# Decoder layer on one core: keys and values of a batch projected by shared 512-column products

## What is computed

```python
def attn(h):                                   # h = layernorm(x)
    q, k, v = h @ q_w.T + q_b, h @ k_w.T + k_b, h @ v_w.T + v_b   # split into 16 heads of 16
    qp, kp = elu(q) + 1, elu(k) + 1
    kv = einsum('bhsd,bhse->bhde', kp, v)
    z = einsum('bhsd,bhd->bhs', qp, kp.sum(axis=2))[..., None]
    return merge(einsum('bhsd,bhde->bhse', qp, kv) / (z + EPS)) @ o_w.T + o_b

x = x + attn(layernorm(x))
x = x + softmax(masked context scores * ...) against layernorm(x)
x = x + ffn(layernorm(x))                      # fwht, silu(gate) * up, fwht, down
```

## Time and profile before

| | us |
|---|---|
| median of 3 runs (lowest, highest) | 125.69 (125.47, 125.76) |
| the profiled execution | 125.14 |
| its span in the trace | 123.3 |
| PE busy | 119.2 (97%) |
| DVE busy | 82.7 (67%) |
| ACT busy | 71.6 (58%) |
| POOL busy | 68.5 (56%) |

### The profile page before, as it was taken

The page is one execution under the profiler, slowest core; times in us unless marked ns, Lnnn a source line. Parts: engine busy times, 40 slices in busy tenths (PEclk is TensorE's granted clock), DMA queues, the critical chain, the costliest instruction groups (busy, mean ns, idle before and its releaser), DMA issues.

```text
span 123.3 us, 2272 instructions
## 1 busy us (share of the span) xinstructions
PE 119.2 (97%) x804; PEld 107.0 (87%) x804; DVE 82.7 (67%) x207; ACT 71.6 (58%) x158; POOL 68.5 (56%) x89
## 2 busy tenths in 40 slices
PE   5999999999999999999999999999999999999990
PEld 2259999999999999999989999988888888889890
DVE  1399989899889899899998959674522332220521
ACT  1785696679748689888491479983135444280000
POOL 2228959979979966959802605762005574066000
DMA  3999910280000000000000110000110000000121
GB/s 123 316 377 423 398 76 5 53 330 3 8 0 0 0 5 3 0 0 0 0 5 0 43 45 0 5 0 0 39 46 3 5 0 0 0 0 0 54 73 43
DMA packets 3823, 7.64 MB, mean 62 GB/s; under 512 B 544, under 2 KB 1952, under 8 KB 3684
## 3 DMA queue, kind: packets, MB, share of 16 engines
q1 hardware_dynamic: 3806, 7.50, 16.8%
q10 hardware_dynamic: 6, 0.01, 0.0%
HBM read 6.46 MB, written 1.05 MB: 61 GB/s over the span
## 4 chain that ended last, share of the span: by engine, by line
PE 97%; POOL 0%; DVE 0%; issue 0%; POOLq 0%
PE bank L1283 19%; PE bank L1295 18%; PE bank L1300 11%; PE bank L1177 10%; PE bank L1304 5%; PE bank L1201 5%; PE bank L1239 5%; PE bank L1155 4%; PE bank L1115 4%; PE bank L1211 3%; PE bank L1221 3%; PE bank L1309 2%; PE bank L1146 2%; PE bank L1247 2%; PE bank L1128 1%; PE bank L1259 1%
## 5 line engine op out<-in xcount | busy, mean ns | idle before, releaser
L1283 PE MATMUL bank<-xh_home,wug 128*128 128x256 f32 x192 | 24.7, 285 | 0.0
L1283 PEld LDWEIGHTS bank<-xh_home,wug 128*128 128x128 f32 x192 | 23.6, 191 | 0.1
L1295 PE MATMUL bank<-xh_home,wug 128*128 128x512 f32 x96 | 22.0, 390 | 0.0
L1295 PEld LDWEIGHTS bank<-xh_home,wug 128*128 128x128 f32 x96 | 18.0, 188 | 3.7
L969 DVE SCALAR_TENSOR_TENSOR back<-bank,sc_up,back 128x512 f32<-128x512 f32 x8 | 6.0, 751 | 15.0 <-PE bank L1295 15.0
L351 POOL TENSOR_TENSOR hs<-back,hs 128x256 fp32r<-128x256 f32 x8 | 5.9, 740 | 17.0 <-ACT hs L614 16.9
L345 POOL TENSOR_TENSOR hs<-front,hs 128x256 fp32r<-128x256 f32 x16 | 11.5, 740 | 6.6 <-ACT hs L599 6.6
L1177 PE MATMUL bank<-watt,xT 128*128 128x256 f32 x96 | 14.0, 288 | 0.0
L1177 PEld LDWEIGHTS bank<-watt,xT 128*128 128x128 f32 x96 | 12.3, 189 | 0.9 <-ACT xT L492 0.7
L606 ACT ACTIVATE back<-bank,vecs 128x512 f32<-128x512 f32 x8 | 5.5, 688 | 12.1 <-PE bank L1295 12.1
L1300 PE MATMUL bank<-wdh,hs 128*128 128x512 f32 x48 | 12.5, 396 | 0.0
(11 more groups left out here) (132 smaller groups left out, 257.6 us busy)
## 6 DMA issues: line engine op xcount, KB each, us to landing
wd_a<-in_w_d SPq DMA_DIRECT2D x1, 1024.0 KB, 8.0
front<-in_w_ug SPq DMA_DIRECT2D x2, 512.0 KB, 8.5
back<-in_w_ug SPq DMA_DIRECT2D x2, 512.0 KB, 3.8
out<-x_res SPq DMA_DIRECT2D x8, 128.0 KB, 1.9
wd_b<-in_w_qkv SPq DMA_DIRECT2D x3, 256.0 KB, 4.5
x_res<-in_x SPq DMA_DIRECT2D x1, 512.0 KB, 6.0
x_res<-in_x_first SPq DMA_DIRECT2D x1, 385.0 KB, 3.1
back<-in_ctx_t SPq DMA_DIRECT2D x1, 260.0 KB
```

What stands on the lines that cost most here:

```text
L1283: ins = mm(dst[:, n * SEQ:(n + 1) * SEQ], wug[:, wa, k, at_col + j * P:at_col + (j + 1) * P], xh[b][:, xb, k, :], start=(i == 0), stop=(i ...
L1295: ins = mm(dst[:, :].rearrange("p (b s) -> p b s", s=SEQ), wug[:, wa, k, at_col + j * P:at_col + (j + 1) * P], xh_home[:, PAIR, cols], sta ...
```

## The change

Keys and values of a batch become one group KV(b) of PE's order. For each of the two token tiles six products take 2 x 256 columns at once (the weights of K and of V side by side), so a bank holds K and V of one tile, where it held K of both tiles or V of both. The group has two neighbouring banks; to address them together the eight banks are now one PSUM tensor. `exp_k` and `elu_k` read the left halves of both banks, `v_add` the right halves. `exp_k` and `v_add` therefore wait for both banks. A bank of KV is free again for the next group when `v_add` is done (semaphore vx), and no longer by a count of the bank's own.

Order: in HEAD, K(b) and V(b) become KV(b) at the place of K(b) for batches 0 to 2, so NUM(b-1) comes behind the values too; KV(3) stands behind XH(0), where K(3) stood ahead of it; Q(1) comes ahead of AT(0). On DVE `v_add(2)` moves ahead of `ln_stats(3, 0)` and `at_lo(1)`. The lists of ACT, POOL and SP are as before.

```diff
-HEAD = (("mx", 0), ("u", 0), ("T1", 0), ("u", 1), ("K", 0), ("V", 0), ("Q", 0), ("T1", 1), ("SC", 0),
-        ("ST", 0), ("K", 1), ("NUM", 0), ("V", 1), ("T1", 2), ("AT", 0), ("Q", 1), ("OUT", 0), ("ST", 1),
...
+HEAD = (("mx", 0), ("u", 0), ("T1", 0), ("u", 1), ("KV", 0), ("Q", 0), ("T1", 1), ("SC", 0),
+        ("ST", 0), ("KV", 1), ("NUM", 0), ("T1", 2), ("Q", 1), ("AT", 0), ("OUT", 0), ("ST", 1),
...
+        bank_of[group], turn_of[group] = b, n // (BANKS - 1)
+        before[group], last[b] = last.get(b), group
+        reads_before[group] = reads[b]
+        reads[b] += group[0] != "KV"
...
         def wait_read(eng, name, i, t=0):
-            eng.wait_ge(read[bank_of[name, i, t]], turn_of[name, i, t] + 1)
+            if name == "KV":
+                eng.wait_ge(s["vx"], i + 1)
+            else:
+                eng.wait_ge(read[bank_of[name, i, t]], reads_before[name, i, t] + 1)
...
             def exp_k(b):
-                wait_full(act, "K", b)
+                for i in range(ST):
+                    wait_full(act, "KV", b, i)
                 if b:
-                    wait_read(act, "K", b - 1)
-                a.activation(ek[:, :], B("K", b)[:, :], ACT.Exp, bias=neg1[:, :]).then_inc(s["ek"], 1)
+                    act.wait_ge(s["kp"], b)
+                a.activation(ek[:, :].rearrange("p (i d) -> p i d", i=ST), both(b, 0), ACT.Exp, bias=neg1[:, :]).then_inc(s["ek"], 1)
...
             softmax(0)
+            v_add(2)
             ln_stats(3, 0)
             at_lo(1)
-            v_add(2)
...
             def take(name, i, t=0):
-                if turn_of[name, i, t]:
-                    pe.wait_ge(read_of(name, i, t), turn_of[name, i, t])
+                if before[name, i, t]:
+                    wait_read(pe, *before[name, i, t])
...
+            def kv_proj(b):
                 pe.wait_ge(s["xT_hi"], b + 1)
                 if b == 0:
-                    pe.wait_ge(s["w_hi"], c + 1)
+                    pe.wait_ge(s["w_hi"], 2)
+                for i in range(ST):
+                    dst = take("KV", b, i)
                     for n, (k, wa, xb) in enumerate(X_PASSES):
...
+                        mm(dst.rearrange("p (c o) -> p c o", c=2), xT[:, b % 2, xb, k, i * P:(i + 1) * P],
+                           wqkv[:, wa, 0:2, k, :], start=(n == 0), stop=(n == len(X_PASSES) - 1))
...
+                    done(mm(dst[:, 0:HID], ones[:, 0:P], bias_r[:, K_COLS], start=False, stop=True, skip_group_check=True), "KV", b, i)
```

More of the change, by code:

```diff
@@ L76, in banks_of @@
 def banks_of(group, i):
-    return [(group, i, t) for t in range(2)] if group in ("NUM", "Y", "GG") else [(group, i, 0)]
+    return [(group, i, t) for t in range(2)] if group in ("NUM", "Y", "GG", "KV") else [(group, i, 0)]
 def schedule():
@@ L97, in decoder_kernel @@
 def decoder_kernel(nc, x_first, x, ctx_t, w_qkv, bias, w_o, w_ug, w_d, vec, row, row_wsd, mask, const, out):
-    bank_of, turn_of = {}, {}
+    bank_of, turn_of, reads_before, before = {}, {}, {}, {}
+    last, reads = {}, [0] * BANKS
     for n, group in enumerate(schedule()):
-        bank_of[group], turn_of[group] = n % (BANKS - 1), n // (BANKS - 1)
+        b = n % (BANKS - 1)
+        bank_of[group], turn_of[group] = b, n // (BANKS - 1)
+        before[group], last[b] = last.get(b), group
+        reads_before[group] = reads[b]
+        reads[b] += group[0] != "KV"
     for b in range(ST):
-        bank_of["SC", b, 0], turn_of["SC", b, 0] = BANKS - 1, b
+        bank_of["SC", b, 0], turn_of["SC", b, 0], reads_before["SC", b, 0] = BANKS - 1, b, b
     stack = ExitStack()
@@ L202, in decoder_kernel @@
         masks = bytes_of[:, TILES * SEQ:(TILES + BATCH + ST) * SEQ]
-        bank = [stack.enter_context(nc.psum_tensor(f"bank{i}", [P, 512], F32)) for i in range(BANKS)]
+        psum = stack.enter_context(nc.psum_tensor("bank", [P, BANKS, 512], F32))
+        bank = [psum[:, i, :] for i in range(BANKS)]
         full = [sem(f"bank_full{i}") for i in range(BANKS)]
@@ L211, in B, with both @@
             return bank[bank_of[name, i, t]]
+        def both(i, c):
+            first_bank = bank_of["KV", i, 0]
+            assert bank_of["KV", i, 1] == first_bank + 1
+            return psum[:, first_bank:first_bank + 2, c * HID:(c + 1) * HID]
         def wait_full(eng, name, i, t=0):
@@ L229, in decoder_kernel @@
                  "ug_hi ug_lo fly pre_hi pre_lo wd wd_hi "
-                 "xT_hi ek eq z_eps z_inv at_hi "
+                 "xT_hi ek kp vx eq z_eps z_inv at_hi "
                  "sx logit prob rsum x2 "
@@ L550, in mix_in @@
                 else:
-                    wait_read(act, "K", BATCH - 1)
+                    act.wait_ge(s["kp"], BATCH)
                 a.activation(mix[:, 0, :], B("T3", b)[:, 0:SEQ], ACT.Copy, scale=vecs[:, V_SUG:V_SUG + 1]).then_inc(s["mix_in"], 1)
@@ L803, in elu_k @@
                     wait_full(dve, "ST", b - 2)
-                v.scalar_tensor_tensor(kp[:, b % 2, :, :].rearrange("p i d -> p (i d)"), ek[:, :], 1.0, B("K", b)[:, :],
-                                       ALU.min, ALU.max).then_inc(read_of("K", b), 1)
+                v.scalar_tensor_tensor(kp[:, b % 2, :, :], ek[:, :].rearrange("p (i d) -> p i d", i=ST), 1.0, both(b, 0),
+                                       ALU.min, ALU.max).then_inc(s["kp"], 1)
             def v_add(b):
-                wait_full(dve, "V", b)
+                for i in range(ST):
+                    wait_full(dve, "KV", b, i)
                 if b == 0:
@@ L815, in v_add @@
                 v.tensor_tensor(vx[:, b % 2, :, 0:P].rearrange("p (i g) e -> p i g e", i=ST),
-                                B("V", b)[:, :].rearrange("p (i g e) -> p i g e", i=ST, g=FB),
+                                both(b, 1).rearrange("p i (g e) -> p i g e", g=FB),
                                 rows[:, 1:2, :].rearrange("p i (g e) -> p i g e", g=FB).to_broadcast([P, ST, FB, P]),
-                                ALU.add).then_inc(read_of("V", b), 1)
+                                ALU.add).then_inc(s["vx"], 1)
             def elu_q(b):
@@ L1163, in turn3 @@
                 turn("T3", b, xn3)
-            def kv_proj(name, b, c):
-                dst = take(name, b)
+            def kv_proj(b):
                 pe.wait_ge(s["xT_hi"], b + 1)
                 if b == 0:
-                    pe.wait_ge(s["w_hi"], c + 1)
+                    pe.wait_ge(s["w_hi"], 2)
                 for i in range(ST):
-                    into = dst[:, i * HID:(i + 1) * HID]
+                    dst = take("KV", b, i)
                     for n, (k, wa, xb) in enumerate(X_PASSES):
                         if b == 0 and i == 0 and wa:
-                            pe.wait_ge(s[f"w_lo{c}"], 1)
+                            pe.wait_ge(s["w_lo0"], 1)
+                            pe.wait_ge(s["w_lo1"], 1)
                         if i == 0 and xb:
                             wait_read(pe, "T1", b)
[L1177 to L1190, removed]
+                        mm(dst.rearrange("p (c o) -> p c o", c=2), xT[:, b % 2, xb, k, i * P:(i + 1) * P],
+                           wqkv[:, wa, 0:2, k, :], start=(n == 0), stop=(n == len(X_PASSES) - 1))
+                    if b == 0 and i == 0:
+                        pe.wait_ge(s["bias"], 1)
+                        pe.wait_ge(s["ones"], 1)
+                    done(mm(dst[:, 0:HID], ones[:, 0:P], bias_r[:, K_COLS], start=False, stop=True, skip_group_check=True), "KV", b, i)
             def q_proj(b):
@@ L1205, in state @@
             def state(b):
-                wait_read(pe, "K", b)
-                wait_read(pe, "V", b)
+                pe.wait_ge(s["kp"], b + 1)
+                wait_read(pe, "KV", b)
                 dst = take("ST", b)
@@ L1372, in down_pair @@
                 done(ins, "Y", b, 1)
-            steps = {"mx": weights_product, "u": project, "T1": turn1, "SC": scores, "K": k_proj, "V": v_proj, "Q": q_proj,
+            steps = {"mx": weights_product, "u": project, "T1": turn1, "SC": scores, "KV": kv_proj, "Q": q_proj,
                      "ST": state, "NUM": numerator, "AT": turn_at, "OUT": o_proj, "T3": turn3, "XH": hadamard_x, "WD": w_down}
```

## The result

| | us |
|---|---|
| before, median of 4 runs (lowest, highest) | 125.58 (125.35, 125.76) |
| after, median of 4 runs (lowest, highest) | 133.50 (131.60, 136.53) |
| after, the profiled execution | 131.68, span 129.9 |
| ratio after to before, 95% interval | 1.048 (1.045 to 1.052) |

The ratio goes by 131.60 and 131.68 us: of the two longer executions, 136.53 us shows a lower mean granted clock (0.959) and 135.32 us does not (0.999), and the kernel before has long ones at an undisturbed clock too (128.47 and 128.85 us at 0.998 and 0.999, beside 125.31 in the session of x5_all). The change is slower by 6.1 us, with 6.2 forecast.

What follows compares the result with a forecast made beforehand. PE was taken to bound the kernel, never waiting in the head. Waits of 6.9 us less 0.7 saved made 6.2, so 125.69 + 6.2 = 131.9 us; own range 131.0 to 132.9, 8 in 10 129.5 to 133.1.

Steps and rivals of the forecast that it cites:

- the walk: Step through PE's list from 8.36 us with predicted durations, giving PE's lateness at six places, 6.12 us at GU(0).
- the gate weights: Behind GU(0): the last low part of these weights on POOL, ready at 57.38, was to add 0.1 us.
- The products: Wide products replacing pairs in KV: 0.4 us saved over 48 pairs, 0.3 in batch 0, together 0.7 us.
- the value taken, 0: Extra time for exp_k, elu_k and v_add reading two banks: 0 to 0.6 us in all, taken as 0.
- places 1 and 2: T1(1) and T1(2) wait for normalise, queued behind exp_k on ACT: PE late 0.47, then 1.23 us.
- place 3: OUT(0), right behind AT(0), waits for at_hi and at_lo: 1.27 us in all, PE late 2.50.
- place 4: AT(1) waits for the bank of KV(2), freed by v_add(2): 1.94 us idle, PE late 4.26.
- places 5 and 6: XH(0) waits for x3_hi and x3_lo, 1.51 us lost; GU(0) waits for xh_lo(0), PE late 6.12.
- A: Rival: the waits in the head stay hidden and only the saving is left, 125.0 us; chance 0.05.
- B: Rival: no difference, one place alone (OUT(0) or XH(0)) uncovers about the 0.7 us saved, 125.7 us; chance 0.03.
- C: Rival: AT(1) is not held, so its wait of 2.0 us falls away, 129.9 us; chance 0.12.
- D: Rival: the clock falls in PE's new gaps in the head, one fall adding 2.1 us, 134.0 us; chance 0.10.

Runs made afterwards that it cites:

- x5_all: Changed kernel with the edits of x1_norm, x2_vadd, x3_kv3 and x4_st1 together, and at_lo(1) ahead of ln_stats(3, 0): 126.72 and 126.80 us where the clock held.
- x1_norm: Changed kernel with only ACT's list altered: normalise(1, 2) ahead of exp_k(1), exp_k(0) behind u_copy and the first negate_mean: 131.67 us.
- x2_vadd: Changed kernel with v_add(2) ahead of softmax(0) on DVE and nothing else: 130.98 us.
- b_gap: Kernel before, with one added wait holding AT(1) until rstd of batch 0's third normalisation: 127.89 us in one of six executions, the others 129.27 to 132.49.
- x1_again: The kernel of x1_norm run once more, unaltered: 130.07 and 130.08 us where the clock held, 131.75 and 135.18 in the other two.
- x3_kv3: Changed kernel with KV(3) back ahead of XH(0), one entry of HEAD moved: 129.56 us.
- x4_st1: Changed kernel with ST(1) between AT(0) and OUT(0) in HEAD: 130.66 us.
- x7_at0: Changed kernel with AT(0) back ahead of Q(1): 130.68 us.
- x8_all_narrow: x5_all with each wide product made as two products of 256 columns into halves of the same bank: 126.87 and 126.88 us at best.

## Why the prediction was right

*The view it rested on.* PE busy 30.00 of 30.00 us meant that nothing could be uncovered for free. After the change all six waits came up where the walk put them, with the releasers it named (ahead of OUT(0) the timeline of the changed kernel names none, and that of x1_norm names `at_hi`). The part behind GU(0) kept its length; the 0.1 us reckoned there for the gate weights did not show. PE's busy share was to be near 0.83 between 14 and 50 us and was 0.88 between 14 and 50.3.

*The products.* Forecast 0.7 us saved. Measured from start to start of the neighbours: KV(0) 3.12 (8.51 to 11.63) for 3.49, the others 3.09, 3.11 and 2.99 for the 3.28, 3.27 and 3.18 of K and V before: 0.9. The walk itself has 0.93 (0.39 in batch 0, 0.20 in KV(1), 0.18 up to SC(3), 0.16 behind T3(0)), and its waits come to 7.05 and the 0.1 behind GU(0); "6.9 less 0.7" has both too small by some 0.2, and the sum of 6.2 stands. The 0.2 are mostly the slower first products of V(1) and V(2), which followed NUM: 1.52 us each where V(3) took 1.43. `exp_k`, `elu_k` and `v_add` take 0.69, 0.67 and 0.68 from two banks as from one: the value taken, 0, was right.

*The places.* GU(0) came at 50.27, forecast 49.81; 0.15 of the 0.46 between is a later start of KV(0) (8.51 for 8.36), a later landing of loads and no part of the change. PE's lateness, forecast and measured: 1.23 and 1.47 behind T1(2), 2.50 and 2.74 at the end of OUT(0), 4.26 and 4.67 at AT(1), 6.12 and 6.58 at GU(0). The gap ahead of AT(1) was to be 1.94 and is 1.85. So close a total as 6.1 for 6.2 is partly luck: between the two profiled executions the difference is 6.5 (131.68 - 125.14), and it shrinks to 6.1 because the median before lies 0.44 above its profiled execution. The runs took the places apart: 1.6 us for places 1 and 2 (forecast 0.86 + 0.96), 0.9 for place 3 with its cover put back (1.27 with all of it), 0.98 of place 4 from one step of DVE, 1.9 for places 5 and 6 (1.51 + 0.41).

*The rivals.* A and B had no support: no place was hidden. C, a wait of AT(1) that isn't there, fell with x2_vadd. D was named and given 0.10. Of the four executions of the changed kernel one shows a lower clock, 136.53 us at 0.959, above the 134.0 that I gave D. The other long one, 135.32, is not D: its clock is 0.999, and what lengthened it stays open. With both in it the plain median, 133.5, lies above the top of my range, 133.1. A single fall cost 1.6 us in x1_norm, less than the 2.1 I gave it; it was the chance that was too small, since three of the five executions of the kernel of x1_norm show a lower clock (0.985 to 0.987). A trace without gaps could not show it; b_gap would have.

## What to carry to other kernels

Where a profile shows one engine busy without a pause and a hand-made order around it, count for each step that is moved what it was lying over: steps that save nothing themselves (V(1) between NUM(0) and T1(2), K(3) between T3(0) and XH(0)) can be worth more than their merger brings. Here K(3) in its old place was worth 1.9 us, and all the shared products of four batches 0.4. Merging two results into one buffer also merges their waits: whoever reads the first half now waits for the second, all that is queued behind that reader waits with it, and the buffer comes free by its last reader. And a gap on PE can cost more than its length, since the clock may fall behind it.

## What the runs showed of the hardware that was not expected

- The granted clock fell to 0.50 behind gaps of 1.32, 1.85 and 2.31 us on PE, but not in each execution of the same kernel: of the six traces with a gap of 1.85 us only x1_norm's shows a fall (after, x1_again, x3_kv3, x4_st1 and x7_at0 held), and b_gap held in one execution of six (127.89). A fall cost about 1.5 us in the traces (1.5 in b_gap, 1.6 in x1_norm).
- `ctx_lo(1)`, one subtraction of 65 x 512 on DVE, took 0.68 us in the changed kernel and 1.52 in x5_all, where it started while GpSimd's `butterfly(0, 1)` ran. The traces point to that neighbour: in the five in which it started well inside the butterfly (x1_norm, x1_again, x5_all, x7_at0, x8_all_narrow) it ended 0.54 to 0.55 us behind the butterfly's end, wherever it had started. In the kernel before it started 0.04 us ahead of the butterfly (22.24 and 22.28); there it took 0.68, and the butterfly 2.89 instead of 2.39. So whichever of the two starts second seems to wait for the other. No run was made for this alone.
